# Two-layer cross-attention on one core: the order of transfers in the second attention's DMA queue

## What is computed

```
h    = concatenate([x, latents], axis=1)            # here x is ctx (64), latents the layer's 512
q    = (latents @ q_w + q_b)                        # (b, 512, 16, 32)
kmat, v = split((h @ kv_w + kv_b))                  # (b, 576, 16, 32) each
attn = softmax(mask(einsum('bkhd,bnhd->bhkn', q, kmat) / 32))
out  = einsum('bhkn,bnhd->bkhd', attn, v) @ out_w + out_b + residual
out  = out + mlp(rmsnorm(out))
```

## Time and profile before

| | us |
|---|---|
| median of 3 runs (lowest, highest) | 1861.58 (1858.43, 1867.19) |
| the profiled execution's own time | 1862.46 |
| its span, first to last instruction | 1860.6 |
| the second attention in it, first key stack to last score | 730 to 1432 |

### The profile page before, as it was taken

How to read it: one execution, slowest core, us unless ns; L and a number is a source line. 1 busy time by engine, 2 the same in 40 slices (tenths; PEclk the granted TensorE clock), 3 DMA queues, 4 the chain that set the end, 5 groups by cost and what they waited for, 6 DMA issues and landing times.

```text
span 1860.6 us, 23089 instructions
## 1 busy us (share of the span) xinstructions
PE 1642.2 (88%) x6993; PEld 1229.6 (66%) x6993; DVE 1009.4 (54%) x1612; ACT 703.4 (38%) x1260; POOL 541.9 (29%) x543
## 2 busy tenths in 40 slices
PE   5778887899999998888988898989886699999998
PEld 4667775667878786555665555655553477787886
DVE  3665565554333335667766766775787455334333
ACT  3433333431111111367556745663667232111111
POOL 2232245404040505133323422341358210404000
PEclk9788898999999998789988999998988799999999
DMA  5011023501010215223123223221221420101011
GB/s 176 1 40 63 23 91 100 177 1 46 0 45 0 91 70 186 68 83 112 61 72 94 87 61 109 65 91 61 95 84 46 151 81 1 46 0 45 0 41 50
DMA packets 60730, 126.13 MB, mean 68 GB/s; under 512 B 10397, under 2 KB 10722, under 8 KB 60642
## 3 DMA queue, kind: packets, MB, share of 16 engines
q1 hardware_dynamic: 53602, 102.08, 16.8%
q0 software_dynamic: 7040, 23.07, 4.1%
HBM read 90.25 MB, written 34.60 MB: 67 GB/s over the span
## 4 chain that ended last, share of the span: by engine, by line
PE 70%; DVE 14%; issue 6%; ACT 4%; DMA 3%; SPq 1%; POOL 0%; ACTq 0%; DVEq 0%; POOLq 0%
PE bank L2064 18%; PE bank L2052 17%; PE bank L1926 5%; DVE RA L1268 4%; PE bank L1961 3%; PE bank L1922 3%; PE bank L2023 3%; DVE FA L1501 3%; PE bank L1976 3%; PE bank L1977 2%; PE bank L1939 2%; PE bank L1748 2%; PE bank L1724 2%; PE bank L1943 2%; PE bank L1799 1%
## 5 line engine op out<-in xcount | busy, mean ns | idle before, releaser
L2064 PE MATMUL bank<-W,RA 128*128 128x512 f32 x1536 | 384.3, 402 | 25.3 <-DVE RA L1268 25.1
L2052 PE MATMUL bank<-RA,W 128*128 (+1 forms) x1536 | 374.7, 396 | 2.7 <-issue 2.3
L2064 PEld LDWEIGHTS bank<-W,RA 128*128 128x128 f32 x1536 | 290.3, 191 | 99.5 <-DVE RA L1268 31.2
L841 POOL TENSOR_TENSOR RA<-FA,RA 128x512 fp32r<-128x512 f32 (+1 forms) x160 | 216.0, 1354 | 423.9 <-ACT FA L1104 423.8
L2052 PEld LDWEIGHTS bank<-RA,W 128*128 128x128 f32 x1536 | 286.9, 188 | 74.9 <-issue 5.9
L1268 DVE TENSOR_TENSOR RA<-FA,RA 128x512 fp32r<-128x512 f32 (+2 forms) x308 | 274.7, 894 | 68.0 <-ACT FA L1104 54.5
L1160 ACT ACTIVATE FA<-bank,cols 128x512 f32<-128x512 f32 x128 | 88.2, 689 | 560.2 <-PE bank L2052 560.1
L1631 DVE CAST RA<-FA 128x512 fp32r<-128x512 f32 x128 | 62.5, 488 | 368.9 <-ACT FA L1160 368.7
L1103 ACT ACTIVATE RA<-bank 128x512 fp32r<-128x512 f32 (+1 forms) x320 | 192.4, 601 | 170.3 <-PE bank L1961 164.6
L1501 DVE TENSOR_REDUCE FA<-bank 128x1 f32<-128x512 f32 x256 | 169.1, 685 | 65.4 <-PE bank L1939 64.1
L1104 ACT ACTIVATE FA<-bank 128x512 f32<-128x512 f32 (+1 forms) x320 | 191.5, 599 | 0.0
(11 more groups left out here) (149 smaller groups left out, 1838.1 us busy)
## 6 DMA issues: line engine op xcount, KB each, us to landing
RA<-k_parts SPq DMA_DIRECT2D x96, 144.0 KB
FA<-after_layer SPq DMA_DIRECT2D x12, 1024.0 KB, 6.2
RA<-q_parts SPq DMA_DIRECT2D x96, 128.0 KB
k_parts<-FA SPq DMA_DIRECT2D x16, 576.0 KB, 3.2
after_att<-FA SPq DMA_DIRECT2D x32, 256.0 KB, 2.1
q_parts<-FA SPq DMA_DIRECT2D x16, 512.0 KB, 2.7
raw<-in_L_xattn_mlp_w_dram POOLq DMA_DIRECT2D x32, 256.0 KB, 3.4
RA<-after_att SPq DMA_DIRECT2D x12, 512.0 KB, 8.6
```

The lines of the kernel that those rows point to most:

```text
L841: pool.tensor_tensor(pl[0:m, r, :], pf[0:m, r, :], ph[0:m, r, :].bitcast(F32), ALU.subtract).then_inc(p_lo_pool, 1)
L2052: op = pe.matmul(bank[FC1_BANK[i]][:, :], W[:, slot, a, k, i * P:(i + 1) * P], yT_[:, ds(b * (2 * KT * S) + (d * KT + k) * S, S)], start=( ...
L2064: op = pe.matmul(bank[4 + t][:, :], gs[:, a, i, t * P:(t + 1) * P], W[:, slot + 1, d, i, :], start=(i == 0 and a == 0 and d == 0), stop=(i ...
```

## The change

`stack` and `pair` take an argument `xs` that picks the query DMAs (0), the key DMAs (1) or both; the mask row goes with the keys. In SP's list for one group the three query stacks of half 0 move ahead of the wait for the key projection and of the key parts; `max_row` comes before the key stacks of half 0 instead of after both stacks of half 0; `sums(4c+2)` comes before `pair(1)` instead of after it. No transfer is added, dropped or resized; a second wait for `s_full` is added with the split of `pair(0)`.

```
-                def stack(nb, c, half):
+                def stack(nb, c, half, xs=(0, 1)):
 
                     to = stacked[c % 2][half]
                     heads = slice(2 * half, 2 * half + 2)
-                    for x, dst_, src_, order_ in ((0, QS, q_parts, (0, 0, 1)), (1, KS, k_parts, (0, 1, 0))):
+                    for x in xs:
+                        dst_, src_, order_ = ((QS, q_parts, (0, 0, 1)), (KS, k_parts, (0, 1, 0)))[x]
...
-                    if c < 2:
+                    if c < 2 and 1 in xs:
...
-                        def pair(half):
+                        def pair(half, xs=(0, 1)):
                             wait_apart(sp, (s_full, at(0, b, BSTEP, NSTEP * c + 2 * (TT + 1) * (half + 1))))
-                            stack(nb, nc_, half)
+                            stack(nb, nc_, half, xs)
...
                         sums(HG * c)
                         if ahead:
+                            pair(0, (0,))
                             wait_apart(sp, (pb_free, at(0, b, USES, use1(f"{pre}KC{nc_}", last) + 1)))
                             parts(1, nb, nc_)
-                            pair(0)
                         sums(HG * c + 1)
                         if not (last and c == G - 1):
                             u = f"R{c + 1}" if c + 1 < G else "nR0"
                             wait_apart(sp, (pb_free, at(0, b, USES, use1(u, last) + 1)))
                             max_row(b if c + 1 < G else b + 1, (c + 1) % G)
                         if ahead:
+                            pair(0, (1,))
+                        sums(HG * c + 2)
+                        if ahead:
                             pair(1)
-                        sums(HG * c + 2)
```

## The result

The changed kernel takes 1836.25 us (median of four, 1831.58 to 1841.25), the kernel before 1864.38 beside it. The ratio is 0.9852, with a 95% interval from 0.9822 to 0.9883. On the 1862.5 of the prediction's sum that is 27.6 us saved (21.8 to 33.2), against 35.4 forecast: faster, and 8 us short of the number. It comes to 1834.9 (1829.3 to 1840.7), inside the range of 1820 to 1835 by 0.1 us.

A forecast was written before the change was run, and what follows sets the result against it. TensorE's waits for the row of maxima, held by SP's queue order, were taken as what the change could shorten. 1862.46 - 23.2 (row) - 13.2 (clock) + 1 (keys) = 1827.1, stated as 1827 us; range 1820 to 1835.

The forecast's parts named there:

- What bounds it: Second attention's group starts: TensorE waits for the row of maxima, held only by SP's queue order; 23.2 us saved.
- the one good start: Start one group earlier in the same trace: queue free, row issued 0.10 us after the copy, TensorE idle 0.41 us.
- The view's line: Score matmul's waits for the row of maxima: 11 times, 29.7 us together, forecast to fall to some 6 us.
- the two short waits: Two of the 11 waits for the row, 0.41 us each, taken as starts of a group 2 in the first three batches.
- The clock behind the wait: First 10 us of groups after long waits: clock returns to near 1.00, saving 13.2 us at 0.35 per us.
- the eight starts: Groups 1 and 3 of the first three batches, 1 and 2 of the last: 26.4 us of waiting, 3.3 each.
- the prediction's own rule: With clock levels 1.2 and 2.4 GHz, an average of 0.77 over 10 us means 2 x 0.23 x 10 = 4.6 us lower.
- The rival in which the clock falls all the same: At the eight starts, 0.4 us of idleness may still lower the clock; time 1840 us, chance 0.14.
- The keys: Half 0's key stacks, issued behind the row, reach TensorE's first key step 0.3 us in time; 1 us lost charged.
- The wait moving to ScalarE: Rival at group starts: ScalarE still busy, stopping TensorE 1 us in each of eight; about 1835 us, chance 0.06.
- nothing happening: Rival: SP is held elsewhere, the row goes out as late, time stays at 1862 us; chance 0.04.
- The early queries: Half 0's query stacks, issued in a pause of SP, are out by 1045.6, delay no key parts and cost nothing.

The follow-up runs named there:

- the pauses filled: Changed kernel plus four and five matmuls nobody reads in group 1's two waits for VectorE, first three batches: 1822.74 us, ratio 0.979.
- filled starts: Kernel before plus 12 matmuls nobody reads ahead of the wait for the row at eight group starts: 1846.74 us, ratio 0.993.
- the second profile: The changed kernel run once more without any edit: 1834.92 us, ratio 0.9842 to the kernel before.
- the first experiment: Kernel before with the row of maxima ahead of all half 0's stacks, sums(4c+2) ahead of half 1's, queries not early: 1874.48 us, ratio 1.0062.

## Why the prediction was right, and where it was off

**What bounds it: right.** The row waited for nothing but the queue's order. Issue 0.10 us after the copy, landing in 1.8, start with about 0.4 idle were forecast from the one good start in the earlier trace rows, and all three were measured. The view's line fell by 23.3 us, 23.2 were forecast. In that count one of the two short waits is the start of the last batch's group 3 and not of a group 2; the sum is the same.

**The clock: right in its price, wrong in its reach; this is the step that failed.** "The clock behind the wait" forecast 13.2 us, as if only the eight starts lowered the clock. Seven of the starts did return to 1.00 and the eighth to 0.95. The price holds as well: in the changed kernel the first group 1 took 37.23 us at 0.82, which by the prediction's own rule is 2 x 0.18 x 37.23 = 13.4 us at the lower level, and with the pauses filled 32.07; 5.16 / 13.4 = 0.39 per us. The second, 34.17 at 0.90 against 31.95, gives 2.22 / 6.8 = 0.33. With filled starts 10.6 us came in group 1 while its time at the lower level went from 32.9 to 6.5 us by the rows shown, 0.40. The prediction took 0.35. But the gain expected in group 1 assumed that a group which starts at full clock keeps it. Of the 37.8 us, 3.4 + 6.2 x 2 = 15.8 lay behind the starts of group 1, 5.5 us of the 13.2; the 15.8 went and 17 more came in the middle, so that the three groups took 1.7 us longer instead, and filling the two pauses brought 12.5 in the windows. The starts of group 3 did pay: from such a start to the first score of the next batch it is 70.48, 70.50 and 70.45 us before and 69.28, 68.00 and 69.19 after, 5.0 less, where 4.6 x 3 x 0.35 = 4.8 were forecast. The last batch, for whose two starts 2.9 us were forecast, gave no clock gain: from the start of its group 1 to its last score it has 0.86 in 96.08 us before, 0.84 in 94.91 after and 0.86 in 94.45 in the second profile, though nearly 3 us of waiting had gone. The cause was not tested.

The rival in which the clock falls all the same, at 1840, named 0.4 us of idleness at the starts as the cause, and the groups 1 as the place to doubt. What happened is that rival in part, in that place, by another cause: between 5.8 us (by the medians) and 9.6 us (by the profile) of the 13.2 did not come. 5.5 of that are group 1's, where the stretches begin at the pauses for VectorE, and 2.9 the last batch's. The view of waits of the kernel before had the pauses' line already.

**The keys: mis-sized.** 1 us was charged, 3.1 came. Half 0 was to be there 0.8 + 2.5 = 3.3 us after the first key issue; in the start above it was 1041.94 - 0.14 - 1037.78 = 4.0, with the mask row as its last piece, and TensorE came 0.16 earlier than reckoned, so a margin of 0.3 became a wait of 0.48. The mask row's issue behind the keys had been put at nothing. With it out of the way the key step still waits 2.5 us in all, so most of the wait is the key DMAs' own landing. The Trainium skill's rule to issue a DMA early and wait for it late (page "DMA: Bandwidth & Descriptors", section "Rules for kernel authors") spoke against this part. The trace agrees in kind: 3.1 us in the changed kernel, and 27.4 us, 2.5 at each start, in the first experiment, where the queries go out late too.

**The wait moving to ScalarE, and nothing happening:** no sign of the second. Of the first there is little: the score's waits for ScalarE grew from 7.5 us to 8.8 in the whole program, and the first group 1 has 1.00 and 9.48 us of work in its first 10.

**The early queries: right.** They filled a pause of SP and delayed nothing, since the row's issue is on time everywhere. They were costed at nothing, which is right as a cost, but they are worth 39 us beside the row's move alone (1.0062 against 0.9852), because with them in the queue behind the row the keys are late.

**The sum, by the profile:** 23.3 - 3.1 + 3.6 = 23.8 in the stage, with 3.6 as the remainder, against 23.2 - 1 + 13.2. The medians say 3.8 more, within their interval. That the time lies inside the range is luck in part: the two missed terms together take it 7.8 us from the number, and the range ends 7.9 us from it. Its working also puts the high end at 1843, while the range that was given stops at 1835.

**Open:** what sets how long the clock stays low after the same two pauses. It was longer in the changed kernel than in the one before, short or absent in the kernel with filled starts, and the same in both profiles of the changed kernel. Filling the pauses ended the stretches, so in the changed kernel these need the pauses. The kernel with filled starts, which pauses for 1.18 and 1.34 us and keeps 1.00 in one batch, shows that pauses of this kind don't lower the clock every time. What decides it, and the length of a stretch, is not explained.

## What to carry to other kernels

Where a small transfer that everything waits for shares a list with large ones, look for what in the list could have gone earlier, and move that first: the small one can pass only as much as the next consumer can spare. Before counting the gain of a clock that recovers, look for the next pause of the same engine in the same stretch; a lowered clock that goes in one place can come back in the next. A wait that can't be removed can be filled with matmuls that nobody reads, and that was worth 10 to 12 us in the changed kernel and 13 at the starts of the one before.

## What the hardware showed unexpectedly

Pauses of 1.18 and 1.64 us, 5 us apart in otherwise busy work, went with a granted clock of 0.55 over 15 us. Pauses of 1.18 and 1.34 us, 3.3 us apart, left it at 1.00 in one batch of the kernel with filled starts. The Trainium skill, page "TensorE: Matmul & The Clock Gate", section "A second HAM failure mode: psum-queue depth-cycling", describes such a thing for another kernel: short idleness between groups of matmuls, frequent enough, makes the clock swing between its levels. The trace of the changed kernel agrees, though the pauses here are waits for VectorE, and nine matmuls in the pauses kept the clock at 1.00.

An 8 KB row lands in 1.8 us on the list that also carries the large transfers, ahead of them, and in 2.7 at the median and 3.3 at most on another list beside them.
